# Cross-attention and expert FFN on one core: the sums' additions begin with tile 9, half of tiles 10 and 11 is multiplied ahead of the last sums, and the last pair's first projection alternates rows

## The chip, the cores and the metric

The kernel runs on one core of a Trainium2 chip. Its time is the device time of one execution in microseconds (us). It uses five engines with queues of their own, TensorE (PE), VectorE (DVE), ScalarE (ACT), GpSimd (POOL) and SyncE (SP), which wait for each other through semaphores.

## The reference

Eight batches of 56 tokens of width 128 attend, with 16 heads of 64, to 1500 context rows each. An FFN with one expert per batch follows.

```python
kv = context @ Wkv;  k, v = split(kv);  q = layernorm(x) @ Wq           # 16 heads
dots = einsum('bhnd,bhmd->bhnm', q, k) * SCALE
dots = dots - (1.0 - mask)[:, None, :, None] * 1e6
attn = softmax(dots, axis=-1)
x = x + (einsum('bhnm,bhmd->bhnd', attn, v) -> b n (h d)) @ Wout + bout
h = gelu(einsum('etd,edf->etf', layernorm(x), w1) + b1)                  # expert e: batch e
x = x + einsum('etf,efd->etd', h, w2) + b2
```

All is float32, and the time lies in the attention.

## The kernel before, in words

The weights are folded first: Wq with Wk, and Wv with Wout, so that the scores of a batch are products of 896 queries (16 heads x 56 tokens, split in two halves of 448 columns, `CH`) with the context itself. The context of a batch is cut into 12 tiles of 125 rows (`TM`, `MT`). `iteration` stands once in each engine's program and runs for each batch; batches 1 to 6 are a hardware loop of three rounds of two, batch 0 and batch 7 (the last) stand outside.

For each tile t, PE computes the scores into PSUM (`scores`, L439, three terms of split float32), ACT takes the exponential into a buffer `ex(t)` (`exponentials`, L697) and seeds the next scores' bank with the softmax shift (L715), and two tiles later PE multiplies the exponentials with the context (`probs_ctx`: L479 in plain float32, L472 for tiles 2, 4, 6 and 8 in three split terms), in the order of `PV_ORDER` (tile 5 before 4, 7 before 6, 9 before 8). A float32 product shows as two records in the trace, each with a weight load of its own (PEld). Between these, PE does "jobs" for the next batch (`max_job`, L496, whose column maxima DVE takes at L899; the shift rows, L453) and for the batch before (`sum_jobs`, the projection `y_job`, and the FFN of a pair: `zt_job` L539, `hidden_job` L549, `out_job` L558). A job takes one of two PSUM banks, and its drain on DVE frees it (`job_free`).

The softmax's denominators are sums of the exponentials over all 12 tiles. Tiles 0, 1 and 2 are the heads of three chains (`CHAINS`); POOL issues transfers that add tiles 3 to 8 into them (L1213, `add_by_dma`), tile t into chain t mod 3, so that tile 6, 7 and 8 are the last of chains 0, 1 and 2. DVE then adds, in five instructions of 125x896 (`add_to_sum`, L889): chain 0 + chain 1, + chain 2, + tile 9, + tile 10, + tile 11. `ADD_AT` puts the first at place (10, 2) of the tile loop, the next two at (11, 0), and `ADD_LATE` the last two at (0, 0) of the next batch. In the last batch `LAST_ADD_AT` puts one at (10, 2), two at (11, 0) and one at (11, 1), and the fifth stands at (11, 2). DVE's GELU product of the last pair's first half (L1018) stands at (10, 1). `ex_summed` counts the additions; ACT waits for it before it overwrites a buffer of `ex` in the next batch, and its cast of the sums (L726), at tile 0 of the next batch, waits for all five.

The last pair of batches (6 and 7) is treated by halves. Its first half (batch 6) has its projection `y_job` at (5, 2) of batch 7, with 16 heads one after the other into the same 64 rows of the bank (L529); its `residual` on DVE starts at L977. The second half is at the end and has even heads in the one, odd heads in the other 64 rows (L526); its residual adds both (L974, L975). After the tile loop of batch 7 PE does: the row sums (`sum_jobs`, L509), the products of tiles 10 and 11 (`last_probs_ctx`, L488, two products for each half of the columns), `y_job` of the second half in two parts of 8 heads, `out_job` of the first half, four warming matmuls (L612), and the FFN of the second half. ACT makes the inverse of the sums by logarithm and exponential (L737, L743); DVE drains (L927), refines (L934) and normalises (L948) each half of the heads, which lets PE go on with `y_job`.

Of the kernel before, what the change touches and what calls it, by code (L numbers as in the profile page):

```python
# [32 lines left out]
ALU = mybir.AluOpType  # L33
# [61 lines left out]
def wait(eng, sem, value):  # L95

    if not isinstance(value, int) or value > 0:
        eng.wait_ge(sem, value)


def xattn_ffn(nc, x_pairs, ctx, ctx_t, mask_q, wq_t, wk_t, wv_t, w_out, b_out, w1, b1_t, w2, b2, out):
    B, N, D = out.shape
    M = ctx.shape[1]
    E, _, FF = w1.shape
    TM = 12
    MT = M // TM
    Q = HEADS * N
    QT = Q // P
    CH = Q // 2
# [5 lines left out]
    HP = HEADS // 2  # L115
    TOK = 64
    CHAINS, RING, LAST_DMA = 3, 4, 8
    SUMS = CHAINS - 1 + TM - 1 - LAST_DMA
    SPLIT = [2, 4, 6, 8]
    PV_ORDER = [0, 1, 2, 3, 5, 4, 7, 6, 9, 8, 10, 11]  # L120
    SPLITS, CTX_HI_AT = len(SPLIT), 5
# [22 lines left out]

    ADD_AT = {(10, 2): (0,), (11, 0): (1, 2)}
    ADD_LATE = (3, 4)
    LAST_ADD_AT = {(10, 2): (0,), (11, 0): (1, 2), (11, 1): (3,)}
    GELU_AT = (9, 1)
    BEHIND = 2
    assert all(len(m) == QT * KM and FIRST_SHIFT_AT < m[0] and m[-1] < (TM - 2, 0) for m in MAX_AT)  # L150
# [4 lines left out]
    with ExitStack() as stack:  # L155
# [7 lines left out]
        ctx_sb = sb("ctx_sb", [P, 2, TM, D])  # L163
# [49 lines left out]
        x1 = sb("x1", [P, D])  # L213
# [13 lines left out]
        ps_a = stack.enter_context(nc.psum_tensor("ps_a", [P, 2, 512], F32))  # L227
# [19 lines left out]
        scores_ready, ex_ready = sem("scores_ready"), sem("ex_ready")  # L247
        last_half = sem("last_half")
# [5 lines left out]
        ex_summed, pv_done, att_ready = sem("ex_summed"), sem("pv_done"), sem("att_ready")  # L254
# [11 lines left out]
        def ex(t):  # L266

            return ex_all[:, t if t < CHAINS else CHAINS + (t - CHAINS) % RING, :]
# [5 lines left out]
        def read_by(t):  # L274

            return PV_ORDER.index(t) + 1

        def added_by_dma(eng, b, t):

            adds = LAST_DMA // CHAINS  # L280
            eng.wait_ge(ex_added[t % CHAINS], b.at(16 * adds, 16 * (t // CHAINS)))
# [91 lines left out]
        def _(pe):  # L373
# [106 lines left out]
                                          start=(slot == 0), stop=(slot == TM - 1))  # L480
                mm.then_inc(pv_done, 1)

            def last_probs_ctx(b):

                pe.wait_ge(ex_ready, b.at(TM, TM))
                for c in range(2):
                    for t in (TM - 2, TM - 1):
                        mm = nc.tensor.matmul(ps_a[:, c, 0:CH], ctx_sb[0:MT, b.parity, t, :], ex(t)[0:MT, c * CH:(c + 1) * CH],  # L488
                                              start=False, stop=(t == TM - 1))
                    mm.then_inc(last_half, 1)  # L490

            def max_job(b, k, t):

# [21 lines left out]
            def y_job(pair):  # L515

                bank = job()
                for h in range(HEADS):

                    if h == 0:  # L520
                        pe.wait_ge(att_n_ready, 1 + (pair.at_pair(1, 2) if pair.half is None else B - 1 + pair.half))
                    if h == HP and pair.half == 1:
                        pe.wait_ge(att_n_ready, 1 + B + 1)
                    if pair.half == 1:
                        out_rows = slice(TOK * (h % 2), TOK * (h % 2) + TOK)
                        mm = nc.tensor.matmul(bank[out_rows, 0:D], att_n[:, h, pair.tokens()], w_vo[:, h, :],  # L526
                                              start=(h < 2), stop=(h >= HEADS - 2))
                    else:
                        mm = nc.tensor.matmul(bank[pair.tokens(), 0:D], att_n[:, h, pair.tokens()], w_vo[:, h, :],  # L529
                                              start=(h == 0), stop=(h == HEADS - 1))  # L530
                mm.then_inc(job_ready, 1)
# [34 lines left out]
            def iteration(b, prepare=True, pair=None):  # L566
                def jobs_at(at):
                    if b.off == 0 and at == FIRST_SHIFT_AT:
                        shift_jobs()
                    if prepare and at == SHIFT_AT:  # L570
                        pe.wait_ge(shift_ready, b.later(1).at(1, 1))
                        shift_jobs()
                    if b.off == 0 and at in FOLD_AT:
                        fold_vo_jobs(FOLD_AT.index(at))
                    if b.off > 0 and at == SUM_AT:
                        sum_jobs(b.later(-1))
                    if prepare and at in MAX_AT[b.parity]:
                        k, t = divmod(MAX_AT[b.parity].index(at), QT)
                        if t == 0:
                            pe.wait_ge(ctxt_hi_in[k], b.at(16, 16))  # L580
                        if (k, t) == (0, 0):
                            pe.wait_ge(qk_hi_ready, b.later(1).at(1, 0))
                        max_job(b.later(1), k, t)
                    if pair is not None:
                        for place, do in ((Y_AT, y_job), (ZT_AT, zt_job), (HID_AT, hidden_job)):
                            if at == place:
                                do(pair)
                        if at == OUT_AT and prepare:
                            out_job(pair)

                for t in range(TM):
                    scores(b, t, lambda: jobs_at((t, 0)))
                    jobs_at((t, 1))
                    if t >= 2:
                        probs_ctx(b, t - 2, lambda: jobs_at((t, 2)))
                    elif b.off > 0:
                        probs_ctx(b.later(-1), TM - 2 + t, lambda: jobs_at((t, 2)))
                    else:
                        jobs_at((t, 2))
# [60 lines left out]
            jobs.leave()  # L660
            last = Batch(None, B - 1)
            iteration(last, prepare=False, pair=Pair(None, ROUNDS, half=0))
            sum_jobs(last)
            last_probs_ctx(last)
            pair = Pair(None, ROUNDS, half=1)
            y_job(pair)
            out_job(Pair(None, ROUNDS, half=0))
# [8 lines left out]
        def _(act):  # L676
# [3 lines left out]
            def exponentials(b, t):  # L680

                src = ps_s[0:MT, t % 2, :, 0:CH]
                act.wait_ge(scores_ready, b.at(TM, t + 1))

                if b.i is None and b.off == 0 and t == 0:
                    act.wait_ge(rows_cleared, 16)
                if t < CHAINS:
                    wait(act, ex_summed, b.at(SUMS, max(t, 1) - SUMS))
                elif t < CHAINS + RING:
                    before = max(s for s in range(CHAINS, TM) if (s - t) % RING == 0)  # L690
                    wait(act, pv_done, b.at(TM, read_by(before) - TM))
                    if before > LAST_DMA:
                        wait(act, ex_summed, b.at(SUMS, CHAINS - 1 + before - LAST_DMA - SUMS))
                else:
                    act.wait_ge(pv_done, b.at(TM, read_by(t - RING)))
                    added_by_dma(act, b, t - RING)
                nc.scalar.activation(half(ex(t)[0:MT, :]), src, ACT.Exp, scale=SCALE).then_inc(ex_ready, 1)  # L697
# [162 lines left out]
        def _(dve):  # L860
# [15 lines left out]

            def add_to_sum(b, n):

                dst = ex_sum[0:MT, b.parity, :]
                if n < CHAINS - 1:  # L880
                    for j in range(n + 2):
                        added_by_dma(dve, b, LAST_DMA - CHAINS + 1 + j)
                    left, part = ex(0)[0:MT, :] if n == 0 else dst, ex(n + 1)[0:MT, :]
                else:
                    t = LAST_DMA + n - CHAINS + 2
                    dve.wait_ge(ex_ready, b.at(TM, t + 1))
                    left, part = dst, ex(t)[0:MT, :]
                wait(dve, ex_summed, b.at(SUMS, n))
                nc.vector.tensor_tensor(dst, left, part, ALU.add).then_inc(ex_summed, 1)  # L889

            def ex_low_part(b, n):

# [77 lines left out]
            def residual(pair):  # L970
                r = pair.tokens()
                bank = filled()
                if pair.half == 1:
                    step(nc.vector.tensor_tensor(x1[r, :], bank[r, 0:D], pair.pick(x_tok)[r], ALU.add))  # L974
                    nc.vector.tensor_tensor(x1[r, :], bank[0:TOK, 0:D], x1[r, :], ALU.add).then_inc(job_free, 1)  # L975
                else:
                    nc.vector.tensor_tensor(x1[r, :], bank[r, 0:D], pair.pick(x_tok)[r], ALU.add).then_inc(job_free, 1)  # L977
                dve.wait_ge(job_free, jobs.value())
                step(nc.vector.bn_stats(stats[r, 0, :], x1[r, :]))
                nc.vector.tensor_tensor(x2[r, :], x1[r, :], pair.pick(b2_sb)[r], ALU.add)  # L980
                step(nc.vector.bn_aggr(meanvar[r, 0, :], stats[r, 0, :]))
                nc.vector.tensor_scalar(veps[r, 0:1], meanvar[r, 0, 1:2], LN_EPS, None, ALU.add).then_inc(var_ready, 1)
                step(nc.vector.tensor_scalar(half_veps[r, 0:1], meanvar[r, 0, 1:2], LN_EPS, -0.5, ALU.add, ALU.mult))
# [339 lines left out]
```

## Time and profile before

| | |
|---|---|
| median of three timed runs | 381.06 us (379.85 to 382.0) |
| the profiled execution | 381.56 us |
| its span, first to last instruction | 379.6 us |
| its mean granted TensorE clock | 0.991 |
| PE busy | 367.0 us, 97% |
| DVE busy | 278.7 us, 73% |
| ACT busy | 255.1 us, 67% |
| POOL busy | 115.5 us, 30% |

The page tells the busy time of each engine and the chain of work that ended last: at each step it goes back from an instruction to what released it. The trace gives the same in order of time. A granted clock of 1.00 is the full clock of TensorE (2.4 GHz), 0.50 the half (1.2 GHz). Matmul ends are modelled, so starts are safer to read than ends.

### The profile page before, as it was taken

How to read it: one execution, taken by the hardware profiler on the slowest of the kernel's cores; microseconds unless marked ns; L12 is line 12 of the kernel's file. 1: busy time of each engine (PE TensorE's matmuls, PEld its weight loads, DVE VectorE, ACT ScalarE, POOL GpSimd, SP SyncE). 2: the span in 40 equal slices, each digit the busy share in tenths (PEclk: the TensorE clock that was granted, in tenths of full speed). 3: DMA queues.
4: the chain of work that ended last, by engine and by line, in shares of the span. 5: the costliest groups of instructions: out<-in, count | busy, mean ns of one | idle time of the engine just before them, and what ended most of it. 6: DMA issues, size and time to landing. Idle time of an engine off the chain costs nothing.

```text
span 379.6 us, 5788 instructions
## 1 busy us (share of the span) xinstructions
PE 367.0 (97%) x1713; PEld 280.4 (74%) x1713; DVE 278.7 (73%) x456; ACT 255.1 (67%) x334; POOL 115.5 (30%) x125
## 2 busy tenths in 40 slices
PE   7899999999999999999999999999999999999795
PEld 6667777777777787777767887777777887787555
DVE  5888577977797679787698579686789678443653
ACT  3556576797679467796679466887688466958321
POOL 1701562245225341226123431336133330022000
PEclk9999999999999999999999999999999999999988
DMA  7587277348734673359735493279636550377000
GB/s 243 202 191 174 54 145 178 85 116 157 180 82 112 115 179 57 96 130 248 169 96 126 90 205 75 59 164 230 160 92 141 93 100 10 106 147 133 12 2 6
DMA packets 30622, 47.10 MB, mean 124 GB/s; under 512 B 2011, under 2 KB 21371, under 8 KB 30608
## 3 DMA queue, kind: packets, MB, share of 16 engines
q0 software_dynamic: 9936, 27.40, 37.0%
q1 hardware_dynamic: 20672, 19.52, 17.2%
q8 instruction: 8, 0.13, 0.1%
q14 instruction: 6, 0.05, 0.0%
HBM read 24.59 MB, written 0.23 MB: 65 GB/s over the span
## 4 chain that ended last, share of the span: by engine, by line
PE 83%; DVE 10%; issue 3%; DMA 2%; ACT 1%; SPq 1%; DVEq 0%
PE ps_s L439 27%; PE ps_a L479 22%; PE ps_x L496 10%; PE ps_a L472 9%; PE ps_x L529 4%; PE ps_a L416 2%; PE ps_x L549 2%; DMA ctxt_raw<-in_ctx_t 2%; DVE ex_sum L889 2%; DVE shift_diag L910 1%; PE ps_x L453 1%; DVE chunk_max L899 1%; PE ps_x L558 1%; DVE ex_lo L895 1%; PE ps_x L509 1%
## 5 line engine op out<-in xcount | busy, mean ns | idle before, releaser
L899 DVE TENSOR_REDUCE chunk_max<-ps_x 128x1 f32<-128x500 f32 x168 | 110.9, 676 | 31.2 <-PE ps_x L496 28.3
L697 ACT ACTIVATE ex_all<-ps_s 125x896 f32<-125x896 f32 x96 | 88.0, 917 | 46.3 <-PE ps_s L439 44.6
L479 PE MATMUL ps_a<-ex_all,ctx_sb 125*128 125x448 f32 x248 | 110.9, 540 | 0.0
L715 ACT COPY ps_s<-shift_row 125x896 f32<-125x896 f32 x94 | 85.7, 911 | 12.6 <-DVE shift_row L1036 10.0
L496 PE MATMUL ps_x<-ctxt_hi,qk_hi 128*128 128x500 f32 x168 | 80.3, 481 | 1.7 <-DVE chunk_max L899 1.5
L1213 POOL DMA_DIRECT2D ex_all<-ex_all x48 | 42.2, 879 | 117.5 <-ACT ex_all L697 113.3
L439 PE MATMUL ps_s<-qk_hi,ctxt_hi 128*125 128x448 f32 x192 | 76.3, 479 | 0.0
L479 PEld LDWEIGHTS ps_a<-ex_all,ctx_sb 125*128 125x128 f32 x248 | 46.2, 189 | 16.8 <-issue 12.4
L439 PE MATMUL ps_s<-qk_hi,ctxt_lo 128*125 128x448 f32 x192 | 54.8, 367 | 0.0
L439 PE MATMUL ps_s<-qk_lo,ctxt_hi 128*125 128x448 f32 x192 | 54.7, 366 | 0.0
L439 PEld LDWEIGHTS ps_s<-qk_hi,ctxt_hi 128*125 128x125 f32 x192 | 35.9, 187 | 24.5 <-issue 23.4
L895 DVE TENSOR_TENSOR ex_lo<-ex_all,ex_hi 125x896 fp32r<-125x896 f32 x32 | 34.8, 1087 | 16.1 <-ACT ex_hi L705 16.1
L496 PEld LDWEIGHTS ps_x<-ctxt_hi,qk_hi 128*128 128x128 f32 x168 | 31.5, 188 | 16.4 <-DVE chunk_max L899 8.8
L439 PEld LDWEIGHTS ps_s<-qk_hi,ctxt_lo 128*125 128x125 f32 x192 | 35.5, 185 | 4.5
L439 PEld LDWEIGHTS ps_s<-qk_lo,ctxt_hi 128*125 128x125 f32 x192 | 35.6, 185 | 3.4
L889 DVE TENSOR_TENSOR ex_sum<-ex_sum,ex_all 125x896 f32<-125x896 f32 x32 | 34.9, 1090 | 3.4 <-DMA ex_all<-ex_all 2.0
L1203 POOL TENSOR_TENSOR ctxt_lo<-ctxt_raw,ctxt_hi 128x500 fp32r<-128x500 f32 x24 | 34.6, 1446 | 8.8 <-DVE ctxt_hi L916 8.8
L705 ACT CAST ex_hi<-ex_all 125x896 fp32r<-125x896 f32 x32 | 30.0, 937 | 0.0
L1185 POOL TENSOR_TENSOR qk_lo<-qk,qk_hi 128x448 fp32r<-128x448 f32 x16 | 17.9, 1133 | 38.7 <-DVE sum_lo L1041 37.9
L1193 POOL DMA_DIRECT2D ctxt_hi<-in_ctx_t x21 | 12.2, 585 | 50.6 <-PE ps_s L439 49.2
L472 PE MATMUL ps_a<-ex_hi,ctx_lo 125*128 125x448 f32 x64 | 18.9, 377 | 0.0
L472 PE MATMUL ps_a<-ex_hi,ctx_hi 125*128 125x448 f32 x64 | 18.4, 368 | 0.0
(108 smaller groups left out, 385.4 us busy)
## 6 DMA issues: line engine op xcount, KB each, us to landing
ex_all<-ex_all POOLq DMA_DIRECT2D x48, 448.0 KB, 4.5
ctxt_raw<-in_ctx_t SPq DMA_DIRECT2D x8, 750.0 KB, 6.1
ctx_sb<-in_ctx SPq DMA_DIRECT2D x8, 750.0 KB
ctxt_hi<-in_ctx_t POOLq DMA_DIRECT2D x21, 250.0 KB, 3.0
w_sb<-in_w SPq DMA_DIRECT2D x4, 512.0 KB, 4.7
w_sb<-in_w SPq DMA_DIRECT2D x8, 256.0 KB, 6.6
ex_all<-in_wq_t SPq DMA_DIRECT2D x2, 256.0 KB, 3.7
ex_all<-in_wk_t SPq DMA_DIRECT2D x2, 256.0 KB, 4.5
```

Of the source, the lines that this page charges most:

```text
L439: mm = nc.tensor.matmul(dst[c], a[:, u, rows], q[:, u, chunks[c]], start=(n == 0 and not seed), stop=(n == 2 and seed), skip_group_check=seed)
L472: mm = nc.tensor.matmul(ps_a[:, c, 0:CH], a[0:MT, u, n, :], e[0:MT, n % 2, c * CH:(c + 1) * CH], start=False, stop=False)
L479: mm = nc.tensor.matmul(ps_a[:, c, 0:CH], ctx_sb[0:MT, u, t, :], ex(t)[0:MT, c * CH:(c + 1) * CH], start=(slot == 0), stop=(slot == TM - 1))
L496: nc.tensor.matmul(bank[:, 0:MC], qk_hi[:, u, t * P:(t + 1) * P], ctxt_hi[:, u, k * MC:(k + 1) * MC], start=True, stop=True).then_inc(job_ ...
L697: nc.scalar.activation(half(ex(t)[0:MT, :]), src, ACT.Exp, scale=SCALE).then_inc(ex_ready, 1)
L705: nc.scalar.copy(ex_hi[0:MT, n % 2, :], ex(t)[0:MT, :]).then_inc(ex_hi_ready, 1)
L715: nc.scalar.copy(ps_s[0:MT, t % 2, :, 0:CH], half(shift_row[0:MT, b.parity, :])).then_inc(seeded, 1)
L889: nc.vector.tensor_tensor(dst, left, part, ALU.add).then_inc(ex_summed, 1)
L895: nc.vector.tensor_tensor(ex_lo[0:MT, n % 2, :], ex(SPLIT[n])[0:MT, :], ex_hi[0:MT, n % 2, :].bitcast(F32), ALU.subtract).then_inc(ex_lo_r ...
L899: nc.vector.tensor_reduce(chunk_max[:, k, t:t + 1], filled()[:, 0:MC], AX.X, ALU.max).then_inc(job_free, 1)
L1203: nc.gpsimd.tensor_tensor(ctxt_lo[:, b.parity, cols], ctxt_raw[:, cols], ctxt_hi[:, b.parity, cols].bitcast(F32), ALU.subtract).then_inc(c ...
L1213: pool.dma_start(ex(t % CHAINS), ex(t), accum_op=ALU.add).then_inc(ex_added[t % CHAINS], 16)
```

## The change

The additions of a batch get a list, `SUM_PARTS`: chain 0 + tile 9, + chain 1, + tile 10, + chain 2, + tile 11. The counts that ACT waits for before it overwrites a buffer follow from the list (`summed`). In the batches 0 to 6 the places stay. In the last batch two additions stand at (10, 0), ahead of the GELU product, two at (11, 0), and the fifth at (11, 2) as before.

`last_probs_ctx` takes the half of the columns as an argument and waits for tiles 10 and 11 one by one; the first half stands ahead of the last `sum_jobs`, the second behind it. `y_job` and `residual` of the last pair's first half now alternate rows too, with one more addition in `residual`.

```diff
-    SUMS = CHAINS - 1 + TM - 1 - LAST_DMA
+    SUM_PARTS = [9, 1, 10, 2, 11]
+    SUMS = len(SUM_PARTS)
...
-    LAST_ADD_AT = {(10, 2): (0,), (11, 0): (1, 2), (11, 1): (3,)}
+    LAST_ADD_AT = {(10, 0): (0, 1), (11, 0): (2, 3)}
...
+        def summed(t):
+
+            return 1 + (SUM_PARTS.index(t) if t else 0)
...
-            def last_probs_ctx(b):
-
-                pe.wait_ge(ex_ready, b.at(TM, TM))
-                for c in range(2):
-                    for t in (TM - 2, TM - 1):
-                        mm = nc.tensor.matmul(ps_a[:, c, 0:CH], ctx_sb[0:MT, b.parity, t, :], ex(t)[0:MT, c * CH:(c + 1) * CH],
-                                              start=False, stop=(t == TM - 1))
-                    mm.then_inc(last_half, 1)
+            def last_probs_ctx(b, c):
+
+                for t in (TM - 2, TM - 1):
+                    pe.wait_ge(ex_ready, b.at(TM, t + 1))
+                    mm = nc.tensor.matmul(ps_a[:, c, 0:CH], ctx_sb[0:MT, b.parity, t, :], ex(t)[0:MT, c * CH:(c + 1) * CH],
+                                          start=False, stop=(t == TM - 1))
+                mm.then_inc(last_half, 1)
...
-                    if pair.half == 1:
+                    if pair.half is not None:
                         out_rows = slice(TOK * (h % 2), TOK * (h % 2) + TOK)
...
+            last_probs_ctx(last, 0)
             sum_jobs(last)
-            last_probs_ctx(last)
+            last_probs_ctx(last, 1)
...
-                    wait(act, ex_summed, b.at(SUMS, max(t, 1) - SUMS))
+                    wait(act, ex_summed, b.at(SUMS, summed(t) - SUMS))
...
-                        wait(act, ex_summed, b.at(SUMS, CHAINS - 1 + before - LAST_DMA - SUMS))
+                        wait(act, ex_summed, b.at(SUMS, summed(before) - SUMS))
...
+                t = SUM_PARTS[n]
                 dst = ex_sum[0:MT, b.parity, :]
-                if n < CHAINS - 1:
-                    for j in range(n + 2):
-                        added_by_dma(dve, b, LAST_DMA - CHAINS + 1 + j)
-                    left, part = ex(0)[0:MT, :] if n == 0 else dst, ex(n + 1)[0:MT, :]
+                left = ex(0)[0:MT, :] if n == 0 else dst
+                if n == 0:
+                    added_by_dma(dve, b, LAST_DMA - CHAINS + 1)
+                if t < CHAINS:
+                    added_by_dma(dve, b, LAST_DMA - CHAINS + 1 + t)
                 else:
-                    t = LAST_DMA + n - CHAINS + 2
                     dve.wait_ge(ex_ready, b.at(TM, t + 1))
-                    left, part = dst, ex(t)[0:MT, :]
                 wait(dve, ex_summed, b.at(SUMS, n))
-                nc.vector.tensor_tensor(dst, left, part, ALU.add).then_inc(ex_summed, 1)
+                nc.vector.tensor_tensor(dst, left, ex(t)[0:MT, :], ALU.add).then_inc(ex_summed, 1)
...
-                if pair.half == 1:
+                if pair.half is not None:
+                    other = slice(TOK * (1 - pair.half), TOK * (1 - pair.half) + TOK)
                     step(nc.vector.tensor_tensor(x1[r, :], bank[r, 0:D], pair.pick(x_tok)[r], ALU.add))
-                    nc.vector.tensor_tensor(x1[r, :], bank[0:TOK, 0:D], x1[r, :], ALU.add).then_inc(job_free, 1)
+                    nc.vector.tensor_tensor(x1[r, :], bank[other, 0:D], x1[r, :], ALU.add).then_inc(job_free, 1)
```

## Rows read from the trace of the kernel before

**Rows 1.** The page's first part: busy time, share of the span, instructions.
```profile
PE 367.0 (97%) x1713; PEld 280.4 (74%) x1713; DVE 278.7 (73%) x456; ACT 255.1 (67%) x334; POOL 115.5 (30%) x125
```
**Rows 2.** Stretches: length, busy us by engine, then PEclk, DMA share, GB/s.
```profile
core 0: us, PE busy (x) PEld busy (x) DVE busy (x) ACT busy (x) POOL busy (x), PEclk, DMA share, GB/s
339.00:356.00 17.00, 17.00 (x75) 13.16 (x75) 8.35 (x20) 11.88 (x17) 2.61 (x3) 1.00 0.54 100
360.00:362.00 2.00, 2.00 (x4) 1.00 (x3) 0.00 (x0) 0.86 (x2) 0.00 (x0) 0.50 0.00 0
363.00:366.00 3.00, 3.00 (x14) 1.42 (x14) 2.24 (x4) 0.66 (x2) 0.00 (x0) 1.00 0.00 0
374.00:376.00 2.00, 1.73 (x9) 1.44 (x7) 0.58 (x3) 1.25 (x3) 0.00 (x0) 0.50 0.00 0
```
**Rows 3.** The chain that ended last, in order of time: start, length, what.
```profile
341.06 1.50 PE ps_a L479 x4
...
350.28 0.93 ACT ex_all L697
...
358.13 1.10 DVE ex_sum L889
```
**Rows 4.** Timeline, both projections: start, length, instruction, idle time before it.
```profile
335.18 3.47 PEld L529 LDWEIGHTS ps_x<-w_vo,att_n 128*64 128x64 f32 x32 [0.65 <-issue]
...
338.81 1.02 PE L479 MATMUL ps_a<-ex_all,ctx_sb 125*128 125x448 f32 x2
...
366.88 0.85 PEld L526 LDWEIGHTS ps_x<-w_vo,att_n 128*64 128x64 f32 x16 [0.35 <-DVE att_n L948]
...
367.80 1.04 PE L558 MATMUL ps_x<-w_sb,w_qk 128*64 128x128 f32 x8
```
**Rows 5.** Timeline: tile 6's exponential, L974 of the chain, transposition, hidden product.
```profile
341.10 0.92 ACT L697 ACTIVATE ex_all<-ps_s 125x896 f32<-125x896 f32 x1 [0.51 <-PE ps_s L439]
...
368.02 0.31 DVE x L974
...
371.01 0.24 PE L539 MATMUL ps_x<-ident,z 64*128 64x64 f32 x1 [1.08 <-DVE z L988]
...
371.61 1.08 PE L549 MATMUL ps_x<-z_t,w_sb 128*128 128x64 f32 x8 [0.36 <-DVE z_t L992]
```
**Rows 6.** Timeline: GELU product and additions on DVE, exponentials of tiles 10 and 11.
```profile
352.85 0.90 ACT L697 ACTIVATE ex_all<-ps_s 125x896 f32<-125x896 f32 x1
...
352.98 0.42 DVE L1018 TENSOR_TENSOR w_qk<-w_qk 128x256 f32<-128x256 f32 x1 [1.94 <-ACT w_qk L771]
...
354.54 4.68 DVE L889 TENSOR_TENSOR ex_sum<-ex_sum,ex_all 125x896 f32<-125x896 f32 x4
...
355.45 0.92 ACT L697 ACTIVATE ex_all<-ps_s 125x896 f32<-125x896 f32 x1 [1.70 <-PE ps_s L439]
```
**Rows 7.** Timeline: PE's row sums in the last batch.
```profile
359.27 3.23 PE L509 MATMUL ps_x<-ex_sum,ones 125*128 125x448 f32 x4 [2.63 <-DVE ex_sum L889]
```
**Rows 8.** Timeline: tile 8's transfer; DMA issues from 332 to 352 us.
```profile
348.17 0.87 POOL L1213 DMA_DIRECT2D ex_all<-ex_all  x1 [1.97 <-ACT ex_all L697]
...
ex_all<-ex_all POOLq DMA_DIRECT2D x6, 448.0 KB, 4.2
```
**Rows 9.** Timeline: the relay behind the row sums.
```profile
361.11 0.54 ACT L737 ACTIVATE log_sum<-ps_x 128x448 f32<-128x448 f32 x1 [4.74 <-PE ps_x L509]
...
364.35 0.62 DVE L948 TENSOR_TENSOR att_n<-ps_a,inv_sum 128x448 f32<-128x448 f32 x1 [0.70 <-PE ps_a L488]
...
366.20 0.62 DVE L948 TENSOR_TENSOR att_n<-ps_a,inv_sum 128x448 f32<-128x448 f32 x1
```
**Rows 10.** Timeline: the passage from the fourth to the fifth batch.
```profile
180.60 0.88 POOL L1213 DMA_DIRECT2D ex_all<-ex_all  x1 [0.90 <-ACT ex_all L697]
...
189.51 2.22 DVE L889 TENSOR_TENSOR ex_sum<-ex_sum,ex_all 125x896 f32<-125x896 f32 x2 [1.21 <-DMA ex_all<-ex_all]
...
193.74 0.92 PE L479 MATMUL ps_a<-ex_all,ctx_sb 125*128 125x448 f32 x2
...
195.03 0.50 PE L496 MATMUL ps_x<-ctxt_hi,qk_hi 128*128 128x500 f32 x1 [0.37 <-DVE chunk_max L899]
```
**Rows 11.** Timeline: a gap of PE near the start.
```profile
13.35 0.47 PE L496 MATMUL ps_x<-ctxt_hi,qk_hi 128*128 128x500 f32 x1 [1.09 <-DVE chunk_max L899]
```

## The prediction

> **What bounds the kernel now.** The page's busy shares come first: TensorE (PE) is busy for 97% of the span, VectorE (DVE) for 73%, ScalarE (ACT) for 67% [rows 1]. So an edit pays if it takes time out of PE's queue, or out of the part at the end where PE is not the bound. The table of stretches says where that part begins: from 339 to 356 us PE is busy all the time, and behind it the list of instructions has one long gap of PE [rows 2, 7]. The chain of waits names what holds the end: up to 350 it is PE's own work, then it passes to an exponential of ACT (350.28), ends on DVE with the last of five additions (L889, 358.13 to 359.23), and goes on as a relay between PE, DVE and ACT in small pieces [rows 3]. The third view is the order of time, engine by engine, for the last batch.
>
> A number of the whole: the profiled execution took 381.56 us, 379.6 of them its span; the median of the three timed runs is 381.06 (379.85 to 382.0). The sum is made against 381.56. "0.5%", about what a measurement of this kernel can tell from no change, is 1.9 us.
>
> **Part 1: the half projection on alternating rows.** It is `y_job` for the first half of the last pair, at tile 5 of the last batch. The same 16 heads are in the trace in both forms. Today's form (L529): 32 records start at 335.18, and the next work on PE starts at 338.81, so 3.63 us (their weight loads take 3.47). The other half of the pair already alternates (L526): its second 16 records start at 366.88 and the next line starts at 367.80, 0.92 us, with 0.85 of weight loads [rows 4]. So 32 records take 2 x 0.92 = 1.84, and the saving is 3.63 - 1.84 = 1.79 us of PE time, at full clock in both (1.00 in the nearest stretches [rows 2]). From 339 to 356 PE has no gap [rows 2], so all of it should arrive at the last tile. The bounds are 0 (the rows don't overlap in this place) and 3.63 - 2 x 0.85 = 1.93.
>
> What it adds is one DVE addition of 64x128, waited for: its twin L974 takes 0.31 and 0.02 to the next [rows 5]. It delays the variance that ACT needs (L756, L758), which stand in ACT's queue ahead of the exponential of tile 6. In before ACT stands idle for 0.51 us behind L758 until PE's scores are there, and starts that exponential at 341.10: 0.04 of it is the start itself, so the cover is 0.47 us [rows 5]. The scores come 1.79 earlier and the variance 1.79 - 0.33, so 0.14 us of cover are left. I cost it at nothing. If the cover were gone, the exponential of tile 6 would be some tenths late, and PE multiplies tile 6 only after those of tiles 5, 4 and 7: two tiles of slack.
>
> **Part 2: the additions of the last batch.** I work in the positions of before and take off the 1.79 at the end, since PE leads in this stretch and its followers move along. Before, DVE did the GELU product (L1018, 352.98), which had waited 1.94 for ACT, then five additions, four of them 4.68 us from 354.54 on, the last ending at 359.22 [rows 3, 6]. They needn't have begun there: tile 9's exponential ends at 350.28 + 0.92 = 351.20, tile 10's at 353.75, tile 11's at 355.45 + 0.92 = 356.37 [rows 3, 6]. The transfer that folds tile 8 into chain 2 is issued at 348.17, those of tiles 7 and 6 some 2.8 and 5.5 earlier, and 4.2 us to landing is the middle of this stretch: 352.4, 349.5 and 346.8 [rows 8]. The new order on DVE, behind `ex_lo` (L895, done before tile 9's exponential is):
> - chain 0 + tile 9: 351.24 to 352.33; + chain 1: 352.44 to 353.53.
> - the GELU product, now behind these two: its sigmoid is ready at 352.95, it runs at 353.5 instead of 352.98. Only the output product of the first half waits for it, behind everything counted here: nothing.
> - + tile 10: 353.9 to 355.0; + chain 2: 355.1 to 356.2; + tile 11: ready 356.37, so 356.4 to 357.49.
>
> The sums are ready at 357.49 instead of 359.22. No longer the five additions, but the exponential of tile 11 and one addition behind it set this time.
>
> **Part 3: half of tiles 10 and 11 ahead of the sums.** PE comes back at 359.27 after a gap of 2.63 us [rows 7], so its last product (L472) ended at 356.64; the model of ends adds some 0.16 to an issue (two records of L479 last 0.92 [rows 10] where four in a row take 1.50 [rows 3], 0.75 for two), so the next work could have started at 356.48. Before the gap the clock is 1.00, in the stretch 360:362 it is 0.50, and 1.00 again in 363:366: the lower and the upper of its two levels, 1.2 and 2.4 GHz [rows 2]. So the four records of the row sums (L509) took 3.23 us where four of the same width (L479) take 1.50 at full clock [rows 3, 7]. In the new order PE puts two of the four products of L488 into the gap. They need tile 11 (356.37) and take 4 x 0.375 = 1.50: 356.48 to 357.98. That is 0.49 later than the sums are ready: what is now queued behind these products is the row sums, and they start at 357.98 rather than 359.27. The gap is gone, and I take the clock as 1.00 then, so the first half of the sums is done after 0.92 (two records of L479, as above) at 358.92 instead of 361.11, when ACT takes its logarithm [rows 9]. With 0.02 for ACT's start it is 2.17 us gained.
>
> From there the relay is: logarithm, inverse, DVE drains and refines, and then DVE waits 0.70 for the products of L488, to 364.35 [rows 9]. These are done by 358 in the new order, so the wait goes too, and with it 0.68 us (a start 0.02 after the refinement stays). The second half follows on DVE as before, from L948 at 364.35 to the end of the second L948 at 366.82 [rows 9]; its inverse is ready (four ACT steps of 0.54 to 0.58 from 358.94, to 361.3) before DVE asks (362.0), and the second two products are on PE from 359.5 to 361.0, before L948 wants them at 363.35. What ended at 366.83 thus ends at 363.98: 2.85 us earlier. The rest to the end is unchanged work.
>
> **Part 4: the order of additions in the other seven batches.** The same five additions are issued at the same places; the second chain's and the third chain's places are later, tile 9 and 10 come earlier. The exponentials of tiles 9 and 10 stand in ACT's queue ahead of the seed that waits for the shift copies (L1036), and so do these copies ahead of the first addition in DVE's: in the timeline both exponentials end over 1 us before the first addition at all seven: no wait there. ACT's waits on additions before tiles 0 to 6 are for counts that stand behind the cast of the sums (L726), which waits for all five anyway, or for the first two, which are early. What goes is DVE's wait for a late transfer: 1.21 us at 189.51, for a tile 8 issued at 180.60, which is 8.7 us to landing; there is one more like it, of 0.82 [rows 10]. Behind them the column maxima are late, and PE stood idle 0.37 us before 195.03 by the modelled ends, 0.54 with the 0.16 of above [rows 10], and some 0.12 behind the other. The bounds are 0 (PE waits for something else then) and 0.66; I take 0.30, the middle, as transfers differ from run to run.
>
> **The sum.** 1.79 + 2.85 + 0.30 = 4.94; 381.56 - 4.94 = 376.6 us. From the median it would be 376.1.
>
> **The rivals.**
> (A) The clock falls in the new tail. The gap of 2.63 us goes, but shorter ones come: PE has nothing from 361.0 to 362.1 (waits for the first L948), and from 363.0 to 364.0 (the second). The trace has both outcomes for such gaps: after 1.08 us of idleness before 371.01, a transposition and 0.36 us more, the clock is 0.50 in 374:376 [rows 2, 5]; a gap of 1.09 us near the start is followed by full clock [rows 11]. At half clock the second 8 heads take 0.85 more; the output product behind them (1.04 [rows 4]) and the four warming matmuls (about as long) take 3.8 instead of 1.9, so PE is free at 369.6 where z is ready at 369.1 (371.01 - 2.85 + 0.85 [rows 5]), another 0.5; the transposition 0.2 more. Together 1.6, or 2.6 if the hidden product (1.1) is caught too: 378.2 to 379.2.
> The Trainium skill, "TensorE: Matmul & The Clock Gate", section "A second HAM failure mode: psum-queue depth-cycling", says that a TensorE which idles briefly and often between groups of matmuls goes back and forth between the two clocks and pays at each return. By that the new tail, which trades one gap for two, would be rival A, 378.4 us; the trace shows one fall after short gaps [rows 2, 5] and none after another [rows 11], so it is not decided.
>
> (B) The alternation doesn't do in its place what it does in L526, or its PE time is taken back by ACT: parts 2 to 4 alone, 381.56 - 3.15 = 378.4. Against it: the same shapes (128*64, 128x128) and the same clock. It is also the case that the change doesn't do what it says.
>
> (C) Slower: the third chain's addition now stands ahead of tile 11's in the late place at each batch's start, and ACT's cast of the sums, with the exponential of tile 1 behind it, waits for it. If tile 8's transfer were later than DVE gets there, the delay would be paid at seven boundaries. In the worst one it landed at 189.5, and DVE would get there at about 191.1 (three additions and the cast from 187.2). To cost 4.94 + 1.9 us it would have to be late by 1.0 us at each of seven, that is some 11.5 us to landing every time, where 4.2 is the middle at the end and 8.7 the most seen [rows 8, 10]. It would give 383.5 or more.
>
> (D) Some earlier wait of ACT or DVE in tiles 6 to 11 eats most of parts 1 and 2 alike: 380 to 381.
>
> **Chances.** Forecast 0.60; A 0.26; B 0.06; C 0.03; D 0.05. The likeliest is the forecast, 376.6. Below it, all bounds at their good end and the median as base give 381.06 - 1.93 - 2.85 - 0.66 = 375.6, and the timed runs lie up to 1.2 below their median, of which I allow 0.8: 374.8. Above, A's far end: 379.2. Faster by over 0.5% is forecast, A and B and leaves 0.92; within it 0.05; slower 0.03.
>
> **What the profile after would show.** L529 with 32 records in some 1.8 us; no gap of PE between the last L472 and the row sums, and L509 with records of about 0.4 us at clock 1.00; five additions with the GELU product behind the second, the last ending some 1.1 us after tile 11's exponential; no wait of DVE ahead of the first L948; no wait of an addition for a transfer. L948's second run should end near 362.2 in the span. Wrong would be: a half clock on L509 or on L526 (A), L529 at 3.6 us or PE waiting for ACT in tiles 6 to 9 (B, D), or DVE waiting for transfers at the start of a batch (C).

## The result

The changed kernel takes 376.5 us in the median of four timed runs (375.75 to 376.91), the kernel before 380.94: a ratio of 0.9876, with a 95% interval of 0.9848 to 0.9904. It is 1.2% faster. The profiled execution took 376.91 us, with a span of 375.0; that is 4.65 us less than the profiled execution of before. The forecast was 376.6.

The page's busy times, against [rows 1]: PE has lost 3.4 us, and DVE has one instruction more.

```profile
PE 363.6 (97%) x1713; PEld 279.4 (75%) x1713; DVE 279.3 (74%) x457; ACT 255.1 (68%) x334; POOL 116.1 (31%) x125
```

The timeline of PE in the changed kernel's last batch: start, length, instruction, idle time before it. The lines have moved: L530 is the alternating projection, L484 a plain product, L492 a last product, L513 the row sums, L553 the hidden product.

```profile
334.53 1.97 PE L530 MATMUL ps_x<-w_vo,att_n 128*64 128x128 f32 x32
336.42 1.02 PE L484 MATMUL ps_a<-ex_all,ctx_sb 125*128 125x448 f32 x2
...
354.08 1.67 PE L492 MATMUL ps_a<-ex_all,ctx_sb 125*128 125x448 f32 x4
355.58 1.67 PE L513 MATMUL ps_x<-ex_sum,ones 125*128 125x448 f32 x4
357.08 1.67 PE L492 MATMUL ps_a<-ex_all,ctx_sb 125*128 125x448 f32 x4
359.93 1.09 PE L530 MATMUL ps_x<-w_vo,att_n 128*64 128x128 f32 x16 [1.19 <-DVE att_n L953]
361.69 1.09 PE L530 MATMUL ps_x<-w_vo,att_n 128*64 128x128 f32 x16 [0.66 <-DVE att_n L953]
...
366.43 1.69 PE L553 MATMUL ps_x<-z_t,w_sb 128*128 128x64 f32 x8 [0.36 <-DVE z_t L998]
```

Against [rows 4], the next work after the half projection comes 1.89 us after its start instead of 3.63. Against [rows 7], there is no gap ahead of the row sums, and from their start to the next work it is 1.50 us, where before it was 3.03 (359.27 to 362.30). Two new gaps of 1.19 and 0.66 us stand ahead of the two parts of the last projection. The same stretch on ACT and DVE, answering to [rows 5, 6, 9]:

```profile
338.70 0.92 ACT L702 ACTIVATE ex_all<-ps_s 125x896 f32<-125x896 f32 x1 [0.17 <-PE ps_s L444]
```

```profile
350.09 1.09 DVE L894 TENSOR_TENSOR ex_sum<-ex_sum,ex_all 125x896 f32<-125x896 f32 x1
351.10 0.42 DVE L1024 TENSOR_TENSOR w_qk<-w_qk 128x256 f32<-128x256 f32 x1
351.43 2.28 DVE L894 TENSOR_TENSOR ex_sum<-ex_sum,ex_all 125x896 f32<-125x896 f32 x2
354.00 1.09 DVE L894 TENSOR_TENSOR ex_sum<-ex_sum,ex_all 125x896 f32<-125x896 f32 x1 [0.29 <-ACT ex_all L702]
...
359.16 0.62 DVE L953 TENSOR_TENSOR att_n<-ps_a,inv_sum 128x448 f32<-128x448 f32 x1
```

The GELU product (L1024) stands behind the second addition. The last addition waits 0.29 us for tile 11's exponential, so this exponential sets the sums, and no longer a row of additions. The first normalisation (L953) has no wait ahead of it. ACT still stands idle for 0.17 us ahead of the exponential of tile 6 (338.70); less the 0.04 of a start, as the prediction counts, that is 0.13 us of cover.

One thing is worse than before. The hidden product (L553) takes 1.69 us instead of 1.08 [rows 5]. The stretches of the changed kernel (busy us by engine, then PEclk, DMA share, GB/s) say why: the clock falls in the middle of it.

```profile
355.00:356.00 1.00, 1.00 (x4) 0.44 (x4) 0.10 (x1) 0.00 (x0) 0.00 (x0) 1.00 0.00 0
366.00:367.00 1.00, 0.64 (x5) 0.60 (x5) 0.23 (x1) 0.00 (x0) 0.00 (x0) 0.85 0.00 0
367.00:368.00 1.00, 1.00 (x7) 1.00 (x6) 0.00 (x0) 0.00 (x0) 0.00 (x0) 0.50 0.00 0
```

### The profile page after: what moved, and what is told of

Its sections match the earlier page's. It is cut to its first block, busy times and chain, and to the rows that moved or that the text cites. A ratio compares the mean times of both kernels' runs of the same rounds, so it can differ in the third digit from the quotient of the medians.

```text
span 375.0 us, 5775 instructions
## 1 busy us (share of the span) xinstructions
PE 363.6 (97%) x1713; PEld 279.4 (75%) x1713; DVE 279.3 (74%) x457; ACT 255.1 (68%) x334; POOL 116.1 (31%) x125
## 4 chain that ended last, share of the span: by engine, by line
PE 86%; DVE 8%; DMA 2%; issue 2%; ACT 1%; SPq 1%; DVEq 0%; ACTq 0%
PE ps_s L444 29%; PE ps_a L484 23%; PE ps_x L500 10%; PE ps_a L477 10%; PE ps_x L533 3%; PE ps_a L421 2%; PE ps_x L553 2%; DMA ctxt_raw<-in_ctx_t 2%; PE ps_x L458 1%; DVE shift_diag L915 1%; PE ps_x L562 1%; DVE chunk_max L904 1%; DVE ex_lo L900 1%; PE ps_x L530 1%; PE ps_x L515 1%
## 5 line engine op out<-in xcount | busy, mean ns | idle before, releaser
L484 PE MATMUL ps_a<-ex_all,ctx_sb 125*128 125x448 f32 x248 | 110.9, 541 | 0.0
L484 PEld LDWEIGHTS ps_a<-ex_all,ctx_sb 125*128 125x128 f32 x248 | 46.3, 190 | 17.1 <-issue 12.7
```

The costliest lines, as they stand in the source:

```text
L484: mm = nc.tensor.matmul(ps_a[:, c, 0:CH], ctx_sb[0:MT, u, t, :], ex(t)[0:MT, c * CH:(c + 1) * CH], start=(slot == 0), stop=(slot == TM - 1))
```

## How the runs are measured

Executions differ by about a microsecond before the part of interest begins, so each run is read by two distances in its profile beside its time. "Head" is the time from the first addition of batch 0 to that of batch 6 (65.72 to 315.48 in before). "Tail" is from the start of the half projection to the start of the last output product (335.18 to 376.35 in before: 41.17 us); the last output product itself lies behind it. The kernel before was timed again beside each set of runs, and its four medians are given as a range; each ratio is to the runs of before of the same set.

| kernel | median, us | ratio to before (95%) | head | tail | tail against before |
|---|---|---|---|---|---|
| before | 380.94 to 381.38 | 1 | 249.76 | 41.17 | |
| projection alone | 379.48 | 0.9954 (0.9927 to 0.998) | 250.01 | 39.42 | -1.75 |
| additions alone | 377.65 | 0.9898 (0.9867 to 0.9929) | 248.63 | 38.05 | -3.12 |
| split alone | 380.54 | 0.9971 (0.9937 to 1.0005) | 249.75 | 39.78 | -1.39 |
| order alone | 380.47 | 0.9978 (0.9946 to 1.0009) | 248.47 | 41.12 | -0.05 |
| gap filled only | 380.19 | 0.997 (0.9949 to 0.9991) | 249.52 | 39.77 | -1.40 |
| changed | 376.5 | 0.9876 (0.9848 to 0.9904) | 248.56 | 37.24 | -3.93 |
| changed, again | 376.73 | 0.9882 (0.9859 to 0.9906) | 248.48 | 37.29 | -3.88 |
| changed, gaps filled | 375.61 | 0.9858 (0.9834 to 0.9882) | 248.46 | 36.64 | -4.53 |
| changed, no split | 375.97 | 0.9862 (0.9838 to 0.9887) | 248.62 | 36.31 | -4.86 |
| no split, gaps filled | 375.32 | 0.9846 (0.9826 to 0.9867) | 248.48 | 36.32 | -4.85 |
| changed, cover gone | 376.64 | 0.9869 (0.9843 to 0.9895) | 248.43 | 37.21 | -3.96 |

Head and tail of the changed kernel are together 5.13 us shorter than those of before, where the medians differ by 4.44. The medians of the order alone (0.7 against 1.34) and of the additions alone (3.5 against 4.25) fall short alike. No run here says why, so the distances tell where time was gained, and the medians how much of it arrives.

## Experiment 1: the half projection alone

```diff
-                    if pair.half == 1:
+                    if pair.half is not None:
                         out_rows = slice(TOK * (h % 2), TOK * (h % 2) + TOK)
```

with the second addition in `residual`, as in the change.

> The kernel before with part 1 alone: the half projection and its residual on alternating rows. My theory: the projection takes 1.8 to 1.9 us of PE instead of 3.6, everything behind it moves by 1.75 and the time by 1.75 (about 0.46%), the gap ahead of the row sums and the half clock on them stay as they were. Rival B (its time is taken back by ACT at tile 6, or the rows don't overlap): 0 to 0.3 us.

The chain of waits of this kernel, start, length, what:

```profile
336.32 1.90 PE ps_x L526 x32
```

It takes 1.90 instead of 3.64, the tail is 1.75 shorter, and the median 1.7 lower. Part 1 stands, and B is out. The gap ahead of the row sums and the half clock on them are still there, as expected:

```profile
358.60 3.12 PE L509 MATMUL ps_x<-ex_sum,ones 125*128 125x448 f32 x4 [2.63 <-DVE ex_sum L889]
```

The profiled execution was the longest of its twelve (381.68 us) and shows no gain as a whole: it reached the first addition of batch 0 at 66.53 instead of 65.72, and its last output product, behind the tail, met a fall of the clock and took 1.94 us instead of 1.13 (granted clock 0.50 from 373 on).

## Experiment 2: the additions alone

```diff
+    SUM_PARTS = [9, 1, 10, 2, 11]
...
-    LAST_ADD_AT = {(10, 2): (0,), (11, 0): (1, 2), (11, 1): (3,)}
+    LAST_ADD_AT = {(10, 0): (0, 1), (11, 0): (2, 3)}
```

with `summed` and `add_to_sum` as in the change; `last_probs_ctx` stays whole, behind the row sums.

> The kernel before with the new order and places of the additions (parts 2 and 4), the products of tiles 10 and 11 still all behind the sums. The sums are ready at 357.5 in the positions of before instead of 359.2, which leaves a gap of PE of some 0.9 us instead of 2.6. If a gap of 0.9 leaves the clock up, the row sums take 1.5 us instead of 3.2 and the projection of the second half starts its second part 3.3 us earlier: 3.3 in the tail and 0.3 to 0.65 before it, 3.6 to 3.9 in all, which would make the split of part 3 worth nothing, or a loss of 0.4. If the clock falls in spite of the shorter gap: 1.8 in the tail, 2.1 to 2.4 in all, and the split is what keeps the clock.

PE in its timeline (L514 row sums, L493 last products, L531 the last projection):

```profile
356.19 1.77 PE L514 MATMUL ps_x<-ex_sum,ones 125*128 125x448 f32 x4 [0.91 <-DVE ex_sum L894]
357.80 3.17 PE L493 MATMUL ps_a<-ex_all,ctx_sb 125*128 125x448 f32 x8
360.90 1.09 PE L531 MATMUL ps_x<-w_vo,att_n 128*64 128x128 f32 x16
362.41 1.09 PE L531 MATMUL ps_x<-w_vo,att_n 128*64 128x128 f32 x16 [0.41 <-DVE att_n L953]
```

The gap is 0.91 us, the granted clock is 1.00 from 356 to 372, the row sums take 1.61 to the next start. The tail is 3.12 shorter where 3.3 was expected. So the clock doesn't need the split in this profile: moving the additions closes most of the gap by itself. Of the twelve timed runs eleven lie between 376.96 and 378.09 us, with mean granted clocks of 0.994 to 0.999; one took 380.41 at 0.991, and where its clock fell is not recorded.

## Experiment 3: the split alone

```diff
+            last_probs_ctx(last, 0)
             sum_jobs(last)
-            last_probs_ctx(last)
+            last_probs_ctx(last, 1)
```

> The kernel before with part 3 alone: half of tiles 10 and 11 ahead of the row sums, additions as before. The gap of PE shrinks from 2.6 to 1.3 us. Clock up: row sums 1.5 us, ACT's logarithm 0.9 earlier, and the wait of 0.70 ahead of the first normalisation goes: 1.6 us in all. Clock down: only that wait goes, 0.7 us.

```profile
359.70 1.77 PE L508 MATMUL ps_x<-ex_sum,ones 125*128 125x448 f32 x4 [1.13 <-DVE ex_sum L889]
```

The timeline has a gap of 1.13 us, and the row sums at full clock. The tail is 1.39 shorter (1.6 expected). The timed runs give 0.7 with an interval that takes in nothing and 2.4; it is the distance in the profile that tells.

## Experiment 4: the order alone

```diff
+    SUM_PARTS = [9, 1, 10, 2, 11]
```

with `summed` and `add_to_sum` as in the change, and the places of before in all batches.

> The kernel before with the new order of the additions alone, at the places of before in all eight batches (part 4). My theory: 0.3 us, at most 0.66, from the two late transfers, and no waits of the additions for transfers in the profile. In the last batch nothing: the last addition ends where it did. The rival: the 0.65 us by which the changed kernel stood ahead when the half projection began is only a difference between executions, then 0 here.

The tail doesn't move (0.05), and no addition waits for a transfer any more. The head is 248.47 against 249.76, and it is so in every profile: four kernels with the old order have 249.52 to 250.01, eight with the new one 248.43 to 248.63. The means are 1.24 us apart. As far as the profiled executions go, the rival is out, and so is my 0.30; the timed runs give 0.7 here, with an interval that reaches to nothing. The intervals from batch to batch show where it is, in us:

| batches | 0-1 | 1-2 | 2-3 | 3-4 | 4-5 | 5-6 |
|---|---|---|---|---|---|---|
| before | 38.15 | 44.18 | 39.17 | 44.77 | 39.13 | 44.36 |
| split alone | 38.15 | 44.62 | 39.09 | 44.13 | 39.11 | 44.65 |
| order alone | 37.89 | 44.14 | 39.11 | 44.09 | 39.12 | 44.12 |

Two things go. The first is PE's wait behind a late transfer, as in the prediction, but dearer. The changed kernel's timeline at the passage of [rows 10]:

```profile
194.04 0.92 PE L484 MATMUL ps_a<-ex_all,ctx_sb 125*128 125x448 f32 x2
194.44 0.73 PE L500 MATMUL ps_x<-ctxt_hi,qk_hi 128*128 128x500 f32 x1
195.01 0.92 PE L484 MATMUL ps_a<-ex_all,ctx_sb 125*128 125x448 f32 x2
```

From product to product it is 0.97 us; before it was 1.63 (193.74 to 195.37), so the stall was 0.66 and not 0.54, and the other one some 0.25 and not 0.12 (44.36 against 44.12 in the last column). The other profiles of the old order have three late transfers: in the split alone additions waited 1.05, 0.40 and 1.09 us. The first and the third cost PE about half a microsecond each (the columns 1-2 and 5-6), the 0.40 nothing (44.13 in the column 3-4, as in the new order). The second thing that goes is 0.26 between batches 0 and 1, in all four profiles of the old order and in none of the new. The DVE rows there, of before and of the order alone:

```profile
101.07 1.09 DVE L910 TENSOR_TENSOR shift_diag<-ident,row_max 128x896 fp32r<-128x896 f32 x1 [0.29 <-DVE row_max L908]
```

```profile
101.05 0.17 DVE L913 SCALAR_TENSOR_TENSOR row_max<-row_max,negpen 128x7 f32<-128x7 f32 x1
101.25 1.09 DVE L915 TENSOR_TENSOR shift_diag<-ident,row_max 128x896 fp32r<-128x896 f32 x1
```

DVE starts the shift diagonal 0.29 us late behind its own predecessor, and PE waits for it. Nothing in the order of the additions touches these two instructions. It stands in the first round of the hardware loop: in the second and third round of before the same two instructions start 0.23 and 0.24 us apart instead of 0.46 (184.19 to 184.42, 268.08 to 268.32), and in the order alone 0.20 in all three. The program with the new order is also shorter, 5774 instructions in the profile against 5788. So where the instructions lie in the program is a candidate; no run here tests it, and why the gap is there with the old program and not with the new one stays open.

## Experiment 5: the gap filled only

```diff
+            pe.wait_ge(ex_ready, last.at(TM, TM))
+            keep_clock(10)
             sum_jobs(last)
             last_probs_ctx(last)
```

in the kernel before.

> The kernel before, unchanged but for 10 warming matmuls in PE's gap of 2.6 us ahead of the row sums, behind tile 11's exponential. It takes no work off any path, so what it gains is the clock alone. Theory: the clock stays 1.00, the row sums take 1.5 us instead of 3.2 (ACT's logarithm 0.9 earlier), the products behind them 3.0 instead of 3.3 or more, the first normalisation no longer waits 0.7 but about 0.1: 1.5 us in all. Rival (the clock is not what made the row sums slow): 0, or slower where the warming matmuls are in the way.

```profile
356.39 2.44 PE L612 MATMUL ps_s<-ones 128*128 128x128 f32 x20
359.18 1.77 PE L509 MATMUL ps_x<-ex_sum,ones 125*128 125x448 f32 x4 [0.35 <-DVE ex_sum L891]
360.79 3.17 PE L488 MATMUL ps_a<-ex_all,ctx_sb 125*128 125x448 f32 x8
```

The stretch of the row sums, busy us by engine, then PEclk, DMA share, GB/s:

```profile
359.00:361.00 2.00, 1.82 (x5) 1.06 (x6) 0.13 (x1) 0.67 (x2) 0.00 (x0) 1.00 0.00 0
```

No work was taken away; PE just had no gap longer than 0.35 us here, and the clock is 1.00 where it was 0.50 [rows 2]. The row sums take 1.61 us to the next start instead of 3.03 (359.27 to 362.30), the tail is 1.40 shorter, the time 0.30% (0.09 to 0.51). So the half clock behind the gap was itself worth 1.4 us. The split by itself brings the same (1.39): from the row sums to the last projection's second part it is 6.21 us there and 6.22 here (7.61 in before), so once the clock stays up, half of the products done early brings nothing more.

## Experiments 6 to 8: what the short gaps and the split cost

> The changed kernel itself, beside the three below on one chip: 0.987 to 0.989 of the kernel before. In the profile the hidden product of the tail (L553) stands at full or at half clock as the fall happens to come, 1.1 or up to 2.1 us.

The changed kernel once more. This time the fall came earlier, in its timeline at the last projection:

```profile
361.55 1.72 PE L530 MATMUL ps_x<-w_vo,att_n 128*64 128x128 f32 x16 [0.66 <-DVE att_n L953]
363.05 1.91 PE L562 MATMUL ps_x<-w_sb,w_qk 128*64 128x128 f32 x8
364.89 1.32 PE L616 MATMUL ps_s<-ones 128*128 128x128 f32 x8
366.33 0.24 PE L543 MATMUL ps_x<-ident,z 64*128 64x64 f32 x1
366.94 1.08 PE L553 MATMUL ps_x<-z_t,w_sb 128*128 128x64 f32 x8 [0.36 <-DVE z_t L998]
```

```profile
362.00:365.00 3.00, 3.00 (x21) 2.67 (x19) 1.47 (x7) 0.11 (x1) 0.00 (x0) 0.50 0.02 5
```

The projection's second part and the output product are slow, the hidden product is not. From the second part to the last output product it is 10.12 us, in the first profile of the changed kernel 10.08, in before 9.47. The fall costs 0.6 in either place. Next, warming matmuls in the gaps (the second beside the wait at the half of `y_job`):

```diff
             last_probs_ctx(last, 1)
+            keep_clock(4)
...
+                        keep_clock(2)
...
-            keep_clock(4)
+            keep_clock(7)
             zt_job(pair)
             hidden_job(pair)
-            keep_clock(8)
+            keep_clock(12)
```

> The changed kernel with warming matmuls in PE's gaps of the tail: 4 ahead of the second half's projection, 2 between its two parts, 7 instead of 4 ahead of the transposition, 12 instead of 8 behind the hidden product. If the short gaps make the clock fall in the tail (rival A), the hidden product is at full clock in every execution and the kernel is 0 to 0.6 us faster than the changed one, 0.3 in the median. If the clock doesn't hang on these gaps, no difference; if warming matmuls get in the way of PE's work, up to 0.5 slower.

```profile
360.81 1.09 PE L531 MATMUL ps_x<-w_vo,att_n 128*64 128x128 f32 x16
...
365.54 1.08 PE L554 MATMUL ps_x<-z_t,w_sb 128*128 128x64 f32 x8 [0.36 <-DVE z_t L1000]
...
370.27 1.06 PE L563 MATMUL ps_x<-w_sb,w_qk 128*64 128x128 f32 x8 [0.92 <-DVE w_qk L1026]
```

All at full clock, 9.46 us from the first of these rows to the third, and the tail 0.60 to 0.65 shorter than in the changed kernel. The timed runs go the same way: their mean granted clocks are 0.998 to 1.0, where the eight timed runs of the changed kernel have 0.991 to 0.995, and the median is 1.1 us lower than that of the changed kernel beside them. Rival A was true of the changed kernel.

The changed kernel with the products of tiles 10 and 11 whole and behind the sums again:

```diff
-            last_probs_ctx(last, 0)
             sum_jobs(last)
-            last_probs_ctx(last, 1)
+            last_probs_ctx(last)
```

> The changed kernel without part 3: all products of tiles 10 and 11 behind the row sums again, additions and projection as changed. Theory: PE has a gap of 0.9 us ahead of the row sums, they start 0.4 earlier than in the changed kernel, the clock stays at 1.00 over so short a gap, and the products are done before DVE wants them: 0.4 us faster than the changed kernel. Rival: the clock falls and the kernel is 1.2 to 1.7 slower than the changed one.

```profile
355.04 1.77 PE L514 MATMUL ps_x<-ex_sum,ones 125*128 125x448 f32 x4 [0.91 <-DVE ex_sum L894]
...
361.25 1.09 PE L531 MATMUL ps_x<-w_vo,att_n 128*64 128x128 f32 x16 [0.41 <-DVE att_n L953]
```

The row sums start 0.40 earlier than in the changed kernel beside it (355.44), with nearly the same start of the batch, the second part of the last projection 0.30 earlier. Its gaps are 0.91 and 0.41 instead of 1.19 and 0.66, and the clock stays up until 371.9. The tail is 0.98 shorter than the changed kernel's of the same chip: 0.3 from the order, 0.65 from the clock. The tails of experiments 1 and 2 add up to it: 1.75 + 3.12 = 4.87, measured 4.86.

Without the split and with warming matmuls, here 3 ahead of the row sums and none around the last projection (the edit against the kernel just shown):

```diff
+            pe.wait_ge(ex_ready, last.at(TM, TM))
+            keep_clock(3)
             sum_jobs(last)
             last_probs_ctx(last)
...
-            keep_clock(4)
+            keep_clock(7)
...
-            keep_clock(8)
+            keep_clock(12)
```

> As the one without the split, with 3 warming matmuls in the gap ahead of the row sums, 7 instead of 4 ahead of the transposition and 12 instead of 8 behind the hidden product. Theory: 0.4 us faster than the changed kernel from the order, and up to 0.6 more in executions where the changed kernel has its hidden product at half clock; the spread of its runs should be no wider.

```profile
354.50 1.77 PE L514 MATMUL ps_x<-ex_sum,ones 125*128 125x448 f32 x4 [0.19 <-DVE ex_sum L896]
...
370.19 1.06 PE L563 MATMUL ps_x<-w_sb,w_qk 128*64 128x128 f32 x8 [0.93 <-DVE w_qk L1026]
```

It is the fastest kernel of the study: 375.32 us (374.97 to 375.81), where the changed kernel on the same chip has 376.51 to 377.05. Its tail is no shorter than that without the warming matmuls (36.32 and 36.31); what they add is a guard against the fall. Its five timed runs all have a mean granted clock of 1.0, those without the warming matmuls 0.991 to 0.997. Whether the 0.65 us between the two medians is theirs is open, since the executions differ by as much before the tail.

## Experiment 9: the cover of tile 6 gone

```diff
-                    step(nc.vector.tensor_tensor(x1[r, :], bank[r, 0:D], pair.pick(x_tok)[r], ALU.add))
+                    for _ in range(3 if pair.half == 0 else 1):
+                        step(nc.vector.tensor_tensor(x1[r, :], bank[r, 0:D], pair.pick(x_tok)[r], ALU.add))
```

> The changed kernel with the first addition of the first half's residual done three times instead of once (the same result each time): 0.66 us more ahead of the variance, where 0.17 of cover is left in the changed kernel's profile. Theory: the exponential of tile 6 starts 0.5 us later, and nothing behind it on PE, which has two tiles of slack: 0 in the time, the distance from the projection to the row sums unchanged at 21.0 us. Rival: PE waits for ACT in tiles 8 to 11, and the time is 0.3 to 0.5 longer.

```profile
338.88 0.90 ACT L702 ACTIVATE ex_all<-ps_s 125x896 f32<-125x896 f32 x1
```

```profile
334.33 1.97 PE L530 MATMUL ps_x<-w_vo,att_n 128*64 128x128 f32 x32
...
355.38 1.67 PE L513 MATMUL ps_x<-ex_sum,ones 125*128 125x448 f32 x4
```

The exponential starts 4.55 us after the projection instead of 4.17, so 0.38 later and with no idle time before it; the row sums come 21.05 after the projection in both kernels. What was added to ACT's path there never came through to PE.

## Why the prediction was right, and where it wasn't

**Part 1** was forecast at 1.79 and is 1.75 (experiment 1). Costing the added DVE addition at nothing holds, and for the reason given: the cover left was 0.13 where 0.14 was worked out, and an exponential that comes 0.38 later costs nothing (experiment 9).

**Parts 2 and 3** were forecast at 2.85 up to the last normalisation. From the half projection to the second part of the last one it is 27.16 us instead of 31.70, 4.54 less; without the projection's 1.74 that is 2.80. Both steps behind it were right: tile 11's exponential now sets the sums, and the clock stays up over the row sums. The reading of why was incomplete. The prediction let the split stand for the closing of the gap; experiment 2 shows that the additions close it well enough, and experiment 7 that the split then costs 0.3 us up to the last projection's second part, and has the gaps behind which the clock fell. The sum of part 3 had this in it, as the 0.49 us that the row sums start later than they are ready, but I didn't take the next step and ask what the time would be without the split.

**Part 4** was mis-sized: 0.30 was taken, between bounds of 0 and 0.66. The profiles show 1.24 in the head, of which 0.26 are a gap in DVE's stream that no part of the argument touched, and the rest PE's waits behind late transfers. One failed step is the reading of PE's idle time off modelled ends: the distance from product to product, against an undisturbed passage, gives 0.66 where I had 0.54, and 0.25 where I had 0.12. The other is taking the middle of the bounds. All four profiles of the old order lose 0.7 to 1.2 us to late transfers, at differing places, so the lower bound of 0 did not occur in any.

**The last step**, "the rest to the end is unchanged work", failed by 0.6. That is rival A, at a price of 0.6 instead of 1.6 to 2.6: in the second profile of the changed kernel the clock is 0.50 from 362 to 365, and much of what it slowed there, the four warming matmuls and the first half's output product, had slack. The fall was present in both profiles of the changed kernel and in that of experiment 9. The Trainium skill, "TensorE: Matmul & The Clock Gate", section "A second HAM failure mode: psum-queue depth-cycling", tells of a kernel whose TensorE goes back and forth between its two clocks because it idles briefly and often. Three profiles here agree, with a fall after gaps of 1.19 and 0.66 us; a fourth (split alone) has the same pair without a fall there, and two with gaps of 0.91 and 0.41 (additions alone; changed, no split) have none either.

The total came out right partly by luck, because errors of opposite signs met: between the two profiled executions the head gave 1.20 instead of 0.30, the fall took back 0.6, and the changed one reached batch 0's first addition 0.54 us later than before did (66.26 against 65.72), which is a difference between executions: 1.20 + 1.74 + 2.80 - 0.6 - 0.54 = 4.60, the difference of the spans. That 376.5 stands so near to 376.6 also owes 0.6 us to the base: the forecast took 4.94 off the profiled 381.56, while the median of before is 380.94, and the medians differ by 4.44. Rivals B, C and D are out: the projection is 1.89 us, no addition waits for a transfer, and nothing of parts 1 and 2 was lost in tiles 6 to 11: from the half projection to the row sums it is 24.09 us in before and 20.63 in the changed kernel without the split, 3.46 less; the projection alone gives 1.74 of it (22.35) and the additions alone 1.73 (22.36).

## What to carry to other kernels

Where PE stands idle for one engine's last steps, price the clock behind the gap as well as the gap: here 2.6 us of idleness cost another 1.4 us, which filler matmuls alone brought back. When two edits close the same gap, work out each without the other; the second may only cost. And put an addition that depends on a transfer last among those that are ready, so that its lateness is spent before anyone waits.

## What was not expected of the hardware

A fall of the clock costs by what work it meets: 1.4 us over row sums and the products behind them, 0.6 in either of two places of the tail. Gaps of 1.13 and of 1.19 us lie close together, but the first, before row sums, was followed by full clock (split alone), and the pair of 1.19 and 0.66 by a fall of it in the changed kernel; in the split alone the same pair came without a fall before 372, so the length of the gaps alone doesn't decide it, and what else does stays open. And two neighbouring DVE instructions, unchanged themselves, stood 0.29 us apart with nothing to wait for in the four profiles of the old order, and not in eight others, which all have the new order of additions.
